# Mamba mixer on one core: the convolution of two of eight channel tiles on TensorE, and the softplus scratch in the output buffer of another step

## What is computed

```python
xz = jnp.einsum('bld,ed->ble', xn, in_proj_w)
x_inner, z = jnp.split(xz, 2, axis=-1)
xc = conv1d_depthwise_causal(x_inner, conv_w) + conv_b      # 4 taps per channel, along the tokens
xc = silu(xc)
x_ssm = jnp.einsum('bld,ed->ble', xc, x_proj_w)             # 16 B, 16 C, 1 step
dt = softplus(x_ssm[..., -1:] * dt_w[:, 0] + dt_b)
h = exp(dt * A) * h + (dt * u) * B;  y = sum(h * C) + D * u  # scan over the tokens, u = xc
out = (y * silu(z)) @ out_proj_w.T + residual
```

## Time and profile before

| | |
|---|---|
| runs of the kernel before | 3100.45, 3100.91, 3104.59 us (median 3100.91) |
| profiled execution: time | 3096.32 us |
| profiled execution: span, first to last instruction | 3094.7 us |
| mean granted TensorE clock | 0.885 |
| mixer: turn 0 starts / last turn ends | 508.8 us / about 1723 us |
| busy over the span: PE, DVE, ACT, POOL | 81%, 64%, 45%, 39% |

### The profile page before, as it was taken

One profiled execution on the slowest core, in us unless ns is written; L12 is line 12 of the kernel. 1 busy time (PEld: TensorE's weight loads), 2 busy tenths in 40 slices (PEclk: granted clock), 3 DMA queues, 4 the chain that ended last, 5 costly groups with the idle time before them and its releaser, 6 DMA issues. The chain is left out here.

```text
span 3094.7 us, 47825 instructions
## 1 busy us (share of the span) xinstructions
PE 2494.7 (81%) x17070; PEld 2114.0 (68%) x17071; DVE 1973.7 (64%) x2691; ACT 1387.5 (45%) x3353; POOL 1216.0 (39%) x750
## 2 busy tenths in 40 slices
PE   5999986788888878888886740599999588999986
PEld 4999986777787878878786530244444267777775
DVE  7567325999999999999999360122222257777653
ACT  1332426777777777777776110011111123333332
POOL 3000003666666666666667007300000244444231
PEclk9988978999999999999999865799999778998996
DMA  5700000000000000000010006455555511111000
GB/s 208 299 1 1 1 1 29 29 29 30 29 30 29 30 29 30 29 32 33 35 42 3 7 0 218 129 185 171 186 178 165 161 47 33 47 41 30 8 8 14
DMA packets 63510, 201.48 MB, mean 65 GB/s; under 512 B 12346, under 2 KB 17594, under 8 KB 60474
## 3 DMA queue, kind: packets, MB, share of 16 engines
q1 hardware_dynamic: 25210, 96.31, 9.2%
q0 software_dynamic: 26272, 80.77, 8.3%
q10 hardware_dynamic: 11808, 21.50, 1.8%
HBM read 130.31 MB, written 68.23 MB: 64 GB/s over the span
## 5 line engine op out<-in xcount | busy, mean ns | idle before, releaser
L837 POOL TENSOR_TENSOR m_hs<-m_hs,m_BC 128x1040 f32<-128x1040 f32 x256 | 615.3, 2404 | 335.8 <-DVE m_hs L945 335.8
L757 ACT ACTIVATE m_dA<-m_dt,m_A 128x128 f32<-128x128 f32 x2048 | 616.3, 388 | 270.5 <-DVE m_hs L945 151.7
L636 PE MATMUL m_py<-m_hs,ident 128*128 128x130 f32 x4096 | 564.0, 296 | 168.0 <-POOL m_hs L837 167.8
L636 PEld LDWEIGHTS m_py<-m_hs,ident 128*128 128x128 f32 x4096 | 530.4, 208 | 187.3 <-POOL m_hs L837 184.8
L945 DVE TENSOR_TENSOR_SCAN m_hs<-m_dA,m_own 128x1040 f32<-128x1040 f32 x256 | 593.5, 2318 | 25.8 <-DVE m_own L934 16.0
L934 DVE TENSOR_TENSOR m_own<-m_BC,m_own 128x1040 f32<-128x1040 f32 x256 | 317.7, 1241 | 11.8 <-DVE m_hs L945 3.7
L588 PE MATMUL m_pw<-m_xg,m_w_in 128*128 128x130 f32 x2048 | 260.6, 285 | 49.1 <-DVE m_xc L898 38.0
L588 PEld LDWEIGHTS m_pw<-m_xg,m_w_in 128*128 128x128 f32 x2048 | 250.3, 200 | 54.8 <-DVE m_xc L898 43.4
L1340 PE MATMUL e_pG<-e_w_gu,e_xT 128*128 x656 | 232.8, 498 | 11.0 <-issue 7.4
L1320 POOL DMA_DIRECT2D e_x<-slots x80 | 42.9, 537 | 400.9 <-PE e_pX L1331 394.2
L1340 PEld LDWEIGHTS e_pG<-e_w_gu,e_xT 128*128 128x128 f32 x656 | 118.6, 191 | 90.4 <-issue 23.4
(11 more groups left out here) (274 smaller groups left out, 4644.5 us busy)
## 6 DMA issues: line engine op xcount, KB each, us to landing
m_BC<-xs SPq DMA_DIRECT2D x16, 2080.0 KB, 9.5
slots<-a_zero POOLq DMA_DIRECT2D x48, 512.0 KB, 39.5
e_w_gu<-in_gate_up_w SPq DMA_DIRECT2D x32, 768.0 KB, 5.1
e_x<-slots POOLq DMA_DIRECT2D x82, 256.0 KB, 2.9
slots<-e_y ACTq DMA_DIRECT2D x82, 256.0 KB, 2.3
e_w_d<-in_down_w SPq DMA_DIRECT2D x32, 256.0 KB, 5.6
out_h<-t_ho SPq DMA_DIRECT2D x8, 520.0 KB, 3.3
a_AT<-in_A_cols SPq DMA_DIRECT2D x8, 512.0 KB, 6.9
```

The costliest lines, as they stand in the source:

```text
L636: mm = pe.matmul(py[k % 2][:, 0:MT], ident[:, :], hs[u % NB][:, n, :], start=False, stop=(half == 1 and n == HN - 1))
L757: act.activation(images(dA[u % NB][:, n, :])[:, :, 1:TOK], images(dt[b][:, k, :])[:, :, 1:TOK], ACT.Exp, scale=A[:, at:at + 1]).then_inc(d ...
L837: pool.tensor_tensor(hs[u % NB][:, :, :], hs[u % NB][:, :, :], BC[b][:, ST + half * HN:ST + (half + 1) * HN, :], ALU.mult).then_inc(prod_r ...
```

## The change

The convolution of channel tiles 6 and 7 (`PE_TILES`, the third piece) moves from DVE to PE, for all groups but the first. ACT copies the two projected tiles out of `pw[2]` into `e1` in place of their first taps; PE multiplies them in unit 3 by eight diagonal matrices (one for each tap and tile, set up once by DVE) and sums the taps in `pw[2]`; ACT applies the Silu with the bias straight from there, one operation for each tile, behind the Silu of the other six. The gate's third piece, which is written into the same bank, now waits for that Silu (`u_ready`) in place of `conv_ready`. DVE's third convolution piece is gone. The diagonal matrices take the place of the buffer `ex` in SBUF; the softplus scratch that was there now lies in `y[b]`, the output buffer of the group being prepared, which group g - 1 used before it. So ACT's `steps` waits, before Abs, until both parts of that group's output projection are done, in all turns but the first.

```diff
@@ -437,6 +437,8 @@
 CONV_AT, ADD_AT = 3, 11
+PE_TILES = PIECES[2]
+PE_CONV_AT = 3
 class MambaWeights:
@@ -501,7 +503,7 @@
         y = [sb(f"y{i}", [P, ET, MT]) for i in range(2)]
-        ex = sb("ex", [P, ET, MT])
+        diag = sb("diag", [P, len(PE_TILES) * KC, P])
         e1 = sb("e1", [P, ET, MT])
@@ -526,6 +528,12 @@
         y_ready, out_done, h_ready = map(sem, ("y_ready", "out_done", "h_ready"))
+        diag_set, pe_conv = sem("diag_set"), sem("pe_conv")
+        DT = ET - len(PE_TILES)
+        def dve_tiles(q):
+            return q * DT + len(PE_TILES) if not (isinstance(q, int) and q == 0) else 0
         block = ctx.enter_context(nc.Block())
@@ -571,7 +579,10 @@
                 if side == 1:
-                    pe.wait_ge(conv_ready, q * ET + PIECES[j][-1] + 1)
+                    if j == 2 and not first:
+                        pe.wait_ge(u_ready, q + 1)
+                    else:
+                        pe.wait_ge(conv_ready, dve_tiles(q) + PIECES[j][-1] + 1)
                 elif j == 0:
@@ -588,6 +599,15 @@
                 mm.then_inc(in_done, 1)
+            def conv(q):
+                pe.wait_ge(tap0, (q + 1) * ET)
+                for at in range(len(PE_TILES)):
+                    for s in range(KC):
+                        mm = pe.matmul(images(pw[2][:, at * MT:(at + 1) * MT])[:, :, s:TOK], diag[:, at * KC + s, :],
+                                       images(e1[:, at, :])[:, :, 0:TOK - s], start=(s == 0), stop=(s == KC - 1))
+                mm.then_inc(pe_conv, 1)
             def x_proj(q, b):
@@ -639,6 +659,10 @@
                             in_piece(g + 2, b, 0, u - IN_AT)
+                        if u == PE_CONV_AT:
+                            if first:
+                                pe.wait_ge(diag_set, len(PE_TILES) * KC)
+                            conv(g + 1)
                         if GATE_AT <= u < GATE_AT + NP:
@@ -700,16 +724,28 @@
                 act.activation(scale[:, :, :], scale[:, :, :], ACT.Exp, scale=-0.5).then_inc(scale_ready, 1)
-            def tap_piece(q, b, j):
+            def tap_piece(q, b, j, first=False):
                 act.wait_ge(in_done, q * 2 * NP + j + 1)
+                if j == 2 and not first:
+                    n = len(PE_TILES)
+                    act.activation(e1[:, 0:n, :], pw[j][:, 0:n * MT].rearrange("p (j t) -> p j t", t=MT), ACT.Copy).then_inc(tap0, n)
+                    return
                 for at, e in enumerate(PIECES[j]):
...
                                    scale=conv_w[:, e, KC - 1:KC]).then_inc(tap0, 1)
-            def silus(q, b):
-                act.wait_ge(conv_ready, (q + 1) * ET)
-                act.activation(xc[b][:, :, :], xc[b][:, :, :], ACT.Silu).then_inc(u_ready, 1)
+            def silus(q, b, first=False):
+                if first:
+                    act.wait_ge(conv_ready, ET)
+                    act.activation(xc[b][:, :, :], xc[b][:, :, :], ACT.Silu).then_inc(u_ready, 1)
+                else:
+                    act.wait_ge(conv_ready, dve_tiles(q) + DT)
+                    act.activation(xc[b][:, 0:DT, :], xc[b][:, 0:DT, :], ACT.Silu)
+                    act.wait_ge(pe_conv, q)
+                    for at, e in enumerate(PE_TILES):
+                        silu = act.activation(xc[b][:, e, :], pw[2][:, at * MT:(at + 1) * MT], ACT.Silu, bias=conv_b[:, e:e + 1])
+                    silu.then_inc(u_ready, 1)
                 for j in range(NP):
@@ -724,16 +760,19 @@
                 act.activation(xs[:, :], pw[0][0:XP, 0:MT], ACT.Copy).then_inc(xs_ready, 1)
-            def steps(q, b, first=False):
+            def steps(q, b, first=False, reused=True):
                 act.wait_ge(s_done, q + 1)
...
                 act.wait_ge(x_ready, (q + 1) * ET)
+                ex = y[b]
                 if not first:
                     act.wait_ge(dt_ready, q)
+                if reused:
+                    act.wait_ge(out_done, (q - 1) * 2)
                 act.activation(ex[:, :, :], dt[b][:, :, :], ACT.Abs).then_inc(ln_steps, 1)
@@ -767,7 +806,7 @@
                         if u == STEP_AT:
-                            steps(g + 1, 1 - b)
+                            steps(g + 1, 1 - b, reused=not first)
                             if more:
@@ -779,13 +818,13 @@
             for j in range(NP):
-                tap_piece(0, 0, j)
-            silus(0, 0)
+                tap_piece(0, 0, j, first=True)
+            silus(0, 0, first=True)
             square(1)
...
             root(1)
-            steps(0, 0, first=True)
+            steps(0, 0, first=True, reused=False)
             turn(0, 0, first=True)
@@ -821,7 +860,7 @@
                     pool.wait_ge(log_steps, q * 3 + 1)
-                    pool.tensor_tensor(e1[:, :, :], ex[:, :, :], e1[:, :, :], ALU.subtract).then_inc(log_steps, 1)
+                    pool.tensor_tensor(e1[:, :, :], y[b][:, :, :], e1[:, :, :], ALU.subtract).then_inc(log_steps, 1)
                 elif step == 2:
@@ -889,7 +928,7 @@
                 n = len(PIECES[j])
-                done = (q * ET + PIECES[j][0]) * (KC - 2)
+                done = (dve_tiles(q) + PIECES[j][0]) * (KC - 2)
                 for s in range(1, KC):
@@ -954,7 +993,7 @@
                     if not last:
-                        if CONV_AT <= u < CONV_AT + NP:
+                        if CONV_AT <= u < CONV_AT + NP - 1:
                             conv_piece(g + 1, 1 - b, u - CONV_AT)
@@ -974,6 +1013,9 @@
             scale_x(1, 1)
+            for at, e in enumerate(PE_TILES):
+                for s in range(KC):
+                    dve.tensor_scalar(diag[:, at * KC + s, :], ident[:, :], conv_w[:, e, KC - 1 - s:KC - s], None, ALU.mult).then_inc(diag_set, 1)
             step_input(0, 0, 0)
```

## The result

The changed kernel takes 3212.61 us (median of four runs, 3210.26 to 3225.28) against 3100.73 us before: 1.0366 times the time before, 95% interval 1.0346 to 1.0387. That is slower by 112 us; 3213 was forecast. The profiled execution is the longest of the four, 3225.28 us with a span of 3223.7, so its rows lie about 12 us above the median.

A forecast was written before the change was run, and what follows sets the result against it. The ACT-POOL chain from S, not busy DVE, was taken to bound each turn. Per turn 7.5 + 0.8 clock - 0.3 POOL = 8.0; times 14, + 1 for turn 0, = 113 us, giving 3213 us, range 3183 to 3243.

The forecast's parts named there:

- The reading from the mutual waits: ACT and POOL wait for each other once a turn, 7.3 and 5.7 us, so their chain closes the turn.
- S: The end of the scan of unit 5 in a turn, 842.04 us in turn 4 of the kernel before.
- The convolution off DVE, value 0: Six DVE operations behind S, 1.60 us a turn, go; the path from there is ACT's, so nothing is gained.
- The convolution on PE, cost 0: Eight matmuls, 1.95 us, fit where PE idles 1.93 us after unit 3's sums, so they cost nothing.
- the old gap: PE's idleness of 1.93 us after unit 3's sums, waiting for DVE's second convolved piece, before gate piece 1.
- Silu order, +1.6 us: PE's gate piece 2 waits for ACT's Silus, so the copy of xs and PE's work behind it come 1.6 us later.
- Scratch in y: Abs must wait for the previous group's output projection: 5.8 us too late in turn 4, mean of fourteen turns 6.6.
- The clock: PE's idle gap moves ahead of gate piece 2; the same mean slow-clock loss as today, 0.8 us a turn.
- the rival in which every turn pays: PE at half clock before gate piece 2 every turn, +10 to +12 us a turn, 3241 to 3269 us; chance 0.08.
- POOL's 0.3 us back: POOL's third softplus operation takes its fast value, 2.37 us, with DVE idle, returning 0.3 us a turn.
- at DVE's pace: Up to S the turn runs as fast as DVE does, since its inputs are there.
- Turn 0 and setup: Turn 0 has only the later xs, +1 us; eight diagonal matrices, some 1.7 us, fall in DVE's idle stretch, cost 0.

The follow-up runs named there:

- Run 6: Kernel before with xs taken after unit 10 and the softplus started after unit 11, one unit earlier: 3054.92 us against 3098.75.
- run 4: Changed kernel with early copy of convolved tiles out of PSUM and softplus scratch moved out of y: 3095.88 us against 3102.58 for the kernel before.
- run 2: Changed kernel, but ACT copies the two convolved tiles out of PSUM early and applies Silu to all eight as before: 3191.93 us against 3102.58 before.
- run 1: Kernel before with only the softplus scratch moved into y and ACT waiting for the output projection; convolution on DVE: 3191.49 us against 3102.58.
- run 5: Changed kernel with ten idle matmuls before the wait of PE's gate piece 2: 3202.54 us against 3098.75 for the kernel before.
- run 3: Changed kernel with softplus scratch moved out of y, so Abs needs no wait for the output projection: 3125.84 us against 3102.58 for the kernel before.
- the kernel with the shortened chain: run 4's kernel with Silus, x_proj, spread, xs and softplus each one unit earlier, gate pieces 2 and 3 together: 3036.88 us against 3098.75 before.
- run 9: run 4's kernel plus six dummy DVE multiply-adds in unit 5 of each turn but the last: 3151.05 us against 3101.43 for the kernel before.
- run 11: run 4's kernel plus five dummy DVE multiply-adds a turn in unit 5, one operand from PSUM: 3113.36 us against 3103.10 for the kernel before.

## Why the prediction was right

**What bounds.** The reading from the mutual waits held: of the 8.8 us by which a turn grew in the profiled execution, 8.4 lie between S and Abs. Run 6 makes the kernel before 1.4% faster by starting the chain earlier, with DVE's work untouched; run 4 takes 24 us off DVE and gains 7. That DVE was busy for 93% of the stretch said little about the value of its time.

**The convolution off DVE, value 0.** Nearly right: run 2 equals run 1. In run 4 the time falls by 7 us; the part that shortens unit 12's wait for the scan of unit 8 is worth 10.7 in the traces. The prediction had named that item and then booked only the change's own case, in which xs comes too late for it to matter.

**The convolution on PE, cost 0.** Right: 1.94 us inside the old gap.

**Silu order, +1.6 us.** Right as a mechanism and in size. From S to xs 14.0 us were expected without clock loss; it was 14.0 in run 5, 15.2 in turn 4 with the loss and 14.8 in run 3. Run 5, which has no slow gate piece, is the plain sum of both waits: 5.8 + 1.6 + 0.1 = 7.5 a turn were worked out for it, (3202.5 - 3098.8 - 1) / 14 = 7.3 measured, and its trace has 7.5 between S and Abs. As a whole the part costs 3212.6 - 3191.9 = 21 us beside the other wait (run 2), and 3125.8 - 3095.9 = 30 us without it (run 3 against run 4). It is less beside the other wait because there it also saves something: a slow clock at the spread lengthens Abs's wait, to 8.3 to 8.4 us in ten turns of run 2, and it doesn't come in the changed kernel, where the wait is 6.7 to 7.0 us in all fourteen. As the prediction had it, this loss goes as the one in front of gate piece 2 comes.

**Scratch in y.** The mean of 6.6 us between Abs and the output's end, read from the kernel before, is the wait of run 1: 6.7. By the times all but 0.3 us of it passed into the turn, (3191.5 - 3102.6) / 14 = 6.35; in run 1's trace the fourteen turns are 91.3 us longer for 93.3 us of waiting, 6.5 of 6.7 a turn.

**The clock.** +0.8 a turn was taken from today's mean. Gate piece 2 was slowed in nine of the fifteen turns 0 to 14, not in all; between S and Abs the changed kernel's trace has 373.3 us and run 5's 361.4, which is 0.85 a turn, and by the times filling the gap returns 10 us, 0.7 a turn. So the rival in which every turn pays did not happen. Of the Trainium skill's section "HAM oscillation — how this bites in real kernels" (TensorE: Matmul & The Clock Gate) this holds: a PE that starves between bursts can come back at half clock. That it does so each time, as in the kernel of that section, does not hold here, where the gaps are mostly shorter than that kernel's.

**POOL's 0.3 us back.** The step failed, though it is small: in turn 4 it is 16.5 us from Ln's end to the turn's, as before, and the third softplus operation takes 2.83 us, not 2.37. Over the fourteen turns the time from Abs to the end is 0.06 us a turn shorter. Another 0.2 us a turn that the prediction had put at 0 took the place of this term in run 5: DVE comes to S earlier, 483.4 us from the starts of the turns to S against 485.8.

**The clock before S.** The prediction let a turn run "at DVE's pace" up to S because "its inputs are there". In turns 5, 7 and 11 of the profiled execution they are not: DVE waits for sums that PE makes at half clock. This costs 7.1 us against the kernel before, 0.5 a turn, and stands in no term of the sum. How much of it the other three executions have, no trace shows; the profiled one is 12 us above the median.

**Turn 0 and setup.** +1.8 us against +1. Turn 0 starts 2.3 us later than in the profile of before, but so it does in run 1, which sets up no diagonal matrices, so that is not their cost. The eight matrices took DVE 3.54 us, not 1.7, in a stretch in which it was idle.

**The sum.** 8.0 us a turn were forecast, (3212.6 - 3100.7 - 1) / 14 = 7.9 measured: 7.3 without the clock by run 5, and 0.7 for it. The profiled execution has 8.8. The two waits and the clock behind them, which make up the bulk, were right one by one (8.3 forecast between S and Abs, 8.4 in the trace). That the total is met to 1 us is luck: POOL's term failed, two small ones were missing, and each is sure only to a few tenths of a us a turn, 14 times.

## What to carry to other kernels

An engine at 93% with small waits can stand beside a chain across two other engines that closes each iteration; look for pairs that wait for each other once an iteration before valuing the busy one's time. Moving scratch into a "free" buffer is priced by when its last reader is done against when the writer would start, and both are in the timeline of the kernel before. After relieving an engine, reschedule the chain as well: here the relief was worth 7 us by itself (run 4), and in the kernel with the shortened chain 28 us were lost when a load of that kind was put back.

## What the runs showed of the hardware that was not expected

DVE operations with both operands in SBUF can take several times their length while POOL works. The dummy operations of run 9 had a median of 360 ns and a maximum of 2374; with one operand in PSUM (run 11) the maximum was 360. In run 9:

```profile
L1011 DVE SCALAR_TENSOR_TENSOR m_own<-m_xc,m_conv_w x90: 332/360/2374, 538.2 to 1653.2; 128x128 f32<-128x128 f32 x90
```

```profile
L1011 DVE SCALAR_TENSOR_TENSOR m_own<-m_own,m_conv_w,m_xc x75: 331/359/360, 538.4 to 1616.2; 128x128 f32<-128x128 f32 x75
```

The second row is run 11's. In turn 4 of run 9 the six operations start at 854.92, and POOL's product runs from 855.08 to 857.50. The step input at a turn's end shows it too, 2.46 us in the earlier trace rows for an operation that takes 0.28 elsewhere, and in the changed kernel the scaling of x, thirteen times in the stretch, rose from a mean of 1378 ns to 2668. It now starts just behind the start of a POOL product (turn 5: 998.28, the product from 998.00 to 1000.38) and before it did so near the end of one (turn 4: 875.25, the product from 873.67 to 876.06). That is 16.8 us more in all; the step inputs took 11.6 us less (73.2 to 61.6), so the two together explain about half of DVE's missing relief (12 us less busy instead of 22). The scaling of x, before and after:

```profile
L886 DVE TENSOR_TENSOR m_xg<-m_dev,m_scale 128x520 f32<-128x520 f32 x13 | 17.9, 1378 | 0.0
...
L925 DVE TENSOR_TENSOR m_xg<-m_dev,m_scale 128x520 f32<-128x520 f32 x13 | 34.7, 2668 | 0.0
```

That the two engines share a way to SBUF is what the Trainium skill says (GPSIMD Engine Reference, "8. Key points": contention with DVE instructions that have two SBUF inputs), and the trace agrees; that one operation may lose 2 us to it, about the length of POOL's product of 2.4 us, is this trace's number.
